# First scores of both row halves in one step over two PSUM banks, the next image's products in a shared bank, and a new order of the second part

## What is computed

```python
q, k, v = split(x @ w_qkv)          # 16 heads of 16
q, k = rotary(q), rotary(k)
scores = q @ k.T * 16 ** -0.5       # per head, 256 x 256, later keys masked
x = x + (softmax(scores) @ v) @ w_out
x = x + sum over the two best experts of gate * (norm(x) @ expert_w[e])
```

## Time and profile before

| | us |
|---|---|
| median of the runs (lowest, highest) | 706.92 (705.33, 708.26) |
| the profiled execution | 706.3 |
| its span from first to last instruction | 704.5 |
| TensorE busy | 614.3 |
| VectorE busy | 468.7 |
| ScalarE busy | 347.4 |
| GpSimd busy | 240.5 |

### The profile page before, as it was taken

How to read it: one execution, slowest core, us unless ns; L and a number is a source line. 1 busy time by engine, 2 the same in 40 slices (tenths; PEclk the granted TensorE clock), 3 DMA queues, 4 the chain that set the end, 5 groups by cost and what they waited for, 6 DMA issues and landing times.

```text
span 704.5 us, 20352 instructions
## 1 busy us (share of the span) xinstructions
PE 614.3 (87%) x8800; PEld 495.7 (70%) x8800; DVE 468.7 (67%) x1032; ACT 347.4 (49%) x549; POOL 240.5 (34%) x257
## 2 busy tenths in 40 slices
PE   6758999999999998566899787999999999989867
PEld 5647888898989898454777355676767676757656
DVE  3686878787787777414576455676777776767545
ACT  5445545655556454228885343636363626262610
POOL 1000103401010103316677446364636465534520
PEclk9868999999999999785999787999999999999987
DMA  8113001300000002002111202020202020200000
GB/s 315 31 62 103 3 3 42 113 17 3 18 2 3 2 3 72 1 0 60 57 35 46 76 1 75 3 76 16 76 1 91 17 76 17 76 17 6 12 16 16
DMA packets 18489, 29.26 MB, mean 42 GB/s; under 512 B 2784, under 2 KB 11232, under 8 KB 18400
## 3 DMA queue, kind: packets, MB, share of 16 engines
q1 hardware_dynamic: 18400, 27.97, 12.3%
HBM read 21.66 MB, written 6.29 MB: 40 GB/s over the span
## 4 chain that ended last, share of the span: by engine, by line
PE 41%; DVE 6%; ACT 4%; POOL 2%; issue 2%; DVEq 0%; POOLq 0%; ACTq 0%
PE ps L197 22%; PE ps L1113 4%; PE ps L1188 4%; PE ps L1116 3%; DVE mx L1465 2%; PE ps L1170 2%; PE ps L1018 2%; PE ps L1148 2%; PE ps L1144 1%; DVE st L1404 1%; POOL rstd L1348 1%; POOL hl L1371 1%; DVE cl_moe L1415 1%; ACT tn_mlp L1237 1%; ACT wide L1281 1%
## 5 line engine op out<-in xcount | busy, mean ns | idle before, releaser
L1385 POOL TENSOR_TENSOR e2l<-prob,e2h 128x1536 f16<-128x1536 f32 x32 | 98.9, 3102 | 35.3 <-ACT e2h L1316 35.3
L1465 DVE TENSOR_REDUCE mx<-ps 128x2 f32<-128x512 f32 (+1 forms) x96 | 66.0, 687 | 52.7 <-PE ps L1116 52.0
L197 PE MATMUL ps<-secondh,ch_moe 128*128 128x256 f16 (+1 forms) x320 | 83.1, 267 | 3.5 <-DVE cl_moe L1415 3.0
L197 PE MATMUL ps<-secondh,cl_moe 128*128 128x256 f16 (+1 forms) x320 | 83.2, 267 | 0.0
L197 PE MATMUL ps<-secondl,ch_moe 128*128 128x256 f16 (+1 forms) x320 | 83.0, 266 | 0.0
L517 PE MATMUL ps<-yh,wconvh 128*128 128x240 f16 (+2 forms) x288 | 78.2, 271 | 4.6 <-POOL yl L677 4.6
L677 POOL TENSOR_TENSOR yl<-y,yh 128x128 f16<-128x128 f32 x32 | 12.6, 426 | 192.9 <-ACT yh L625 192.9
L517 PE MATMUL ps<-yh,wconvl 128*128 128x240 f16 (+2 forms) x288 | 78.1, 271 | 0.0
L517 PE MATMUL ps<-yl,wconvh 128*128 128x240 f16 (+2 forms) x288 | 78.0, 271 | 0.0
L1310 ACT ACTIVATE prob<-ps 128x1536 f32<-128x1536 f32 x32 | 46.3, 1446 | 30.1 <-PE ps L1170 24.9
L1556 DVE SCALAR_TENSOR_TENSOR acc<-ps,gate,acc 128x256 f32<-128x256 f32 x112 | 48.2, 477 | 9.5 <-PE ps L197 9.3
(11 more groups left out here) (220 smaller groups left out, 1996.9 us busy)
## 6 DMA issues: line engine op xcount, KB each, us to landing
weights_stage<-in_second SPq DMA_DIRECT2D x6, 684.0 KB, 4.0
qs<-rope_scratch SPq DMA_DIRECT2D x48, 64.0 KB, 2.3
ks<-rope_scratch SPq DMA_DIRECT2D x48, 64.0 KB, 2.3
weights_stage<-in_wconv SPq DMA_DIRECT2D x6, 384.0 KB, 3.8
xw<-in_xw SPq DMA_DIRECT2D x8, 256.0 KB, 3.5
xc<-in_xc SPq DMA_DIRECT2D x8, 256.0 KB, 2.7
rope_scratch<-rh SPq DMA_DIRECT2D x8, 256.0 KB, 2.3
rope_scratch<-rl SPq DMA_DIRECT2D x8, 256.0 KB, 2.3
```

The lines of the kernel that those rows point to most:

```text
L197: last = nc.tensor.matmul(out_ap, lhs[x], rhs[w], start=done == 0, stop=done == n - 1)
L1385: nc.gpsimd.tensor_tensor(el[n % 2][:], prob[n % 2][:], eh[n % 2][:], ALU.subtract).then_inc(e2_lo, 1)
L1465: nc.vector.tensor_reduce(mx[c % 2][:, q0 // P, h0:h0 + len(heads)], bank(1, 1).rearrange("p (h m) -> p h m", m=keys), op=ALU.max, axis=AX ...
```

## The change

Four things. A `maxima` step now takes the same heads of both halves (head h and head h + 8), in turn, into two banks, `bank(1, 0)` and `bank(1, 1)`, with one mask matmul for each; there are six steps for an image instead of twelve. VectorE takes one maximum over both banks, 1024 columns. The products `q`, `r` and `v` move from `bank(1, 0)`: for image 0 they stay there, image 1 uses `bank(0, 0)`, and all later ones share `bank(0, 3)` with the weighed values; TensorE waits ahead of each of these steps, and of `weigh`, until the last content of the bank has been read. The strings of all engines are new. In TensorE's, while image 4 is attended, the order is `o e q u r a e a c e l r x e a i x x a i x a v x a i x x i s x`.

```diff
     "pe": (
-        "ttttmmwmtwnmwntqwnmrtrtmvwnmqwnmrwnaarawnaaaavaaaqaanseaearaaerevaaiaaiaaiaaisoqeuaearacaelxirxeaxai"
-        "avaxaxaiaxaixxsoqeuaeraaacelirxeaxaiaxaxavaxaixaixxsqoeauearaacelrxeaixaiaxaxavaxaiaxxsixoqeuaearaac"
-        "elixxreaxaiaaxavaxaixaixxsoqeuaeraacaerlixeaxxaiaxaxaiaxaxaixvsoeuaeaacaelixeaxaxaixaxaiaxaxaixsoeue"
-        "celxiexxixxixxxixouclxxxxxxxx"),
+        "tttmmtwwmtnmwntqwrnmtrmwntvwqmnwmaarnrawaavannqserraeaeieaiavaaiisoequaearcelrxeaixiaxxvaxaixxixsoeq"
...
@@
         SCORE_BANKS = [((0, 1, 2, 3), P, 0), ((0, 1), TOK, P), ((2, 3), TOK, P)]
+        SCORE_USES = L1HALF // GH * len(SCORE_BANKS)
+
+        def qkv_bank(c):
+
+            return bank(1, 0) if c == 0 else bank(0, 0) if c == 1 else bank(0, 3)
@@
+            value_bank_read, weighed = [None], [0]
+
+            def value_bank_free():
+
+                freed(pe, o2_done, weighed[0])
+                if value_bank_read[0]:
+                    pe.wait_ge(*value_bank_read[0])
+
             def qkv_channels(c):
 
+                if c == 1:
+                    pe.wait_ge(t1_done, B)
+                elif c == 2:
+                    pe.wait_ge(t2_done, B - 1)
+                value_bank_free()
                 freed(pe, v2_lo, c)
                 pe.wait_ge(ln["norm"][QKV], c + 1)
-                to_channels(bank(1, 0), tn[QKV][0]).then_inc(ln["tr"][QKV], 1)
+                to_channels(qkv_bank(c), tn[QKV][0]).then_inc(ln["tr"][QKV], 1)
+                value_bank_read[0] = n2_lo, c + 1
@@
             def maxima(c, n):
 
-                p, gr, b = c % 2, n // 3, n % 3
-                heads, keys, q0 = SCORE_BANKS[b]
+                p = c % 2
+                heads, keys, q0 = SCORE_BANKS[n % 3]
                 if n == 0:
                     if c == 0:
                         pe.wait_ge(rows_zeroed, 8 * 16)
+                        pe.wait_ge(v2_lo, 1)
                     pe.wait_ge(stacked[p], (c // 2 + 1) * 12 * 16)
                     freed(pe, shift_done, c)
                 else:
-                    pe.wait_ge(max2, c * GROUPS * 3 + n)
-                to = bank(1, 1)
+                    pe.wait_ge(max2, c * SCORE_USES + n)
                 for m, h in enumerate(heads):
-                    rows, at = row_half(gr * GH + h)
-                    nc.tensor.matmul(to[:, m * keys:(m + 1) * keys], qs[p][rows, at, q0:q0 + P],
-                                     ks[p][rows, at, 0:keys], start=m == 0, stop=False)
-                diagonal = to.rearrange("p (h m) -> p h m", m=keys)[:, :, keys - P:keys]
-                nc.tensor.matmul(diagonal, identb[:], maskb[:].unsqueeze(1).to_broadcast([P, len(heads), P]),
-                                 start=False, stop=True).then_inc(scores2, 1)
+                    for g in R2:
+                        rows, at = row_half(g * L1HALF + n // 3 * GH + h)
+                        nc.tensor.matmul(bank(1, g)[:, m * keys:(m + 1) * keys], qs[p][rows, at, q0:q0 + P],
+                                         ks[p][rows, at, 0:keys], start=m == 0, stop=False)
+                for g in R2:
+                    diagonal = bank(1, g).rearrange("p (h m) -> p h m", m=keys)[:, :, keys - P:keys]
+                    last = nc.tensor.matmul(diagonal, identb[:], maskb[:].unsqueeze(1).to_broadcast([P, len(heads), P]),
+                                            start=False, stop=True)
+                last.then_inc(scores2, 1)
@@
                 if gr == 0:
                     pe.wait_ge(v2_lo, c + 1)
                 pe.wait_ge(e2_lo, n + 1)
-                freed(pe, o2_done, n)
+                value_bank_free()
@@
             def maxima(c, n):
 
-                gr, b = n // 3, n % 3
-                heads, keys, q0 = SCORE_BANKS[b]
-                h0 = gr * GH + heads[0]
-                dve.wait_ge(scores2, c * GROUPS * 3 + n + 1)
-                nc.vector.tensor_reduce(mx[c % 2][:, q0 // P, h0:h0 + len(heads)],
-                                        bank(1, 1).rearrange("p (h m) -> p h m", m=keys),
+                heads, keys, q0 = SCORE_BANKS[n % 3]
+                h0 = n // 3 * GH + heads[0]
+                dve.wait_ge(scores2, c * SCORE_USES + n + 1)
+                nc.vector.tensor_reduce(by_half(mx[c % 2])[:, q0 // P, :, h0:h0 + len(heads)],
+                                        bank(1, 0, 2).rearrange("p (g h m) -> p g h m", g=2, m=keys),
                                         op=ALU.max, axis=AX).then_inc(max2, 1)
```

More of the change, by code:

```diff
@@ L1083, in rotate @@
                     last = split_products(
-                        nc, bank(1, 0)[:, m * TOK:(m + 1) * TOK],
+                        nc, qkv_bank(c)[:, m * TOK:(m + 1) * TOK],
                         [([w["wqkv"][:, (j * 2 + h) * C + m * P:(j * 2 + h) * C + (m + 1) * P] for w in (hi, lo)],
@@ L1087, in rotate @@
                 last.then_inc(qk2_done, 1)
+                value_bank_read[0] = rope_b, c * 4 + 2 * j + 2
             def values(c):
+                value_bank_free()
                 pe.wait_ge(rope_b, c * 4 + 4)
-                token_product(bank(1, 0), QKV, "wqkv", 4 * C, C).then_inc(v2_done, 1)
+                token_product(qkv_bank(c), QKV, "wqkv", 4 * C, C).then_inc(v2_done, 1)
+                value_bank_read[0] = v2_lo, c + 1
             def row_half(h):
@@ L1132, in attend @@
                         pe.wait_ge(t2_done, B)
+                        pe.wait_ge(v2_lo, 2)
                     pe.wait_ge(shift_done, c + 1)
@@ L1191, in weigh @@
                 last.then_inc(pv2, 1)
+                weighed[0] = n + 1
             def out_channels(c):
@@ L1288, in qkv_channels @@
                 act.wait_ge(ln["tr"][QKV], c + 1)
-                high_part(QKV, bank(1, 0), n2_hi)
+                high_part(QKV, qkv_bank(c), n2_hi)
             def stack(c):
@@ L1301, in values @@
                 nc.scalar.activation(vh[c % 3][:, :, :, 0:L1D],
-                                     bank(1, 0).rearrange("p (t h d) -> p t h d", t=TILES, h=L1H),
+                                     qkv_bank(c).rearrange("p (t h d) -> p t h d", t=TILES, h=L1H),
                                      ACT.Copy).then_inc(v2_hi, 1)
@@ L1438, in qkv_low @@
             def qkv_low(c):
-                low_part(c, QKV, bank(1, 0), n2_hi, n2_lo)
+                low_part(c, QKV, qkv_bank(c), n2_hi, n2_lo)
             def rotate(c, j):
@@ L1444, in rotate @@
                 dve.wait_ge(qk2_done, c * 2 + j + 1)
-                x = bank(1, 0).rearrange("p (m t) -> p m t", m=2)
+                x = qkv_bank(c).rearrange("p (m t) -> p m t", m=2)
                 sin = const("sin").rearrange("p (m t) -> p m t", m=2)
@@ L1455, in values @@
                 dve.wait_ge(v2_hi, c + 1)
[L1456 removed]
+                nc.vector.tensor_tensor(vl[c % 3][:], qkv_bank(c).rearrange("p (t h d) -> p t h d", t=TILES, h=L1H),
                                         vh[c % 3][:, :, :, 0:L1D], ALU.subtract).then_inc(v2_lo, 1)
             def maxima(c, n):
[L1461 to L1466 removed]
+                heads, keys, q0 = SCORE_BANKS[n % 3]
[3 more added lines that the diff above has]
+                                        bank(1, 0, 2).rearrange("p (g h m) -> p g h m", g=2, m=keys),
                                         op=ALU.max, axis=AX).then_inc(max2, 1)
@@ L1473, in shifts @@
                 freed(dve, shift_tr, c)
-                dve.wait_ge(max2, (c + 1) * GROUPS * 3)
+                dve.wait_ge(max2, (c + 1) * SCORE_USES)
                 nc.vector.tensor_tensor(mxh[:], mx[c % 2][:], mx[c % 2][:], ALU.max).then_inc(mx_step, 1)
```

22 lines of the change are left out of this document (11 added, 11 removed).

## The result

The changed kernel takes 674.41 us (median of four runs, 671.33 to 675.64) against 706.66 for the kernel before beside it: a ratio of 0.9541, 95% interval 0.9511 to 0.9572, some 30 to 35 us less. The profiled execution has a span of 671.7 us, 32.8 less than before. I had predicted 680 (669 to 695). Of the five executions in experiment 4, one took 1142.05 us; it is a slow one and stays out of the figures given there.

A forecast was written before the change was run, and what follows sets the result against it. TensorE's queue was taken to bound whole images, waits and a lowered clock the start; 10.4 + 1.7 + 5 x 2.4 + 2.4 = 26.5 us off 706.9 gives 680.4, forecast 680, range 669 to 695.

The forecast's parts named there:

- step 1: Score steps on TensorE: both row halves run at once, so 6.84 us an image becomes 4.34, 2.5 less.
- step 2: Maxima on VectorE: 8.3 us an image becomes 7.3; a step following at once waits 1.32 us instead of 0.79.
- that rival: Reductions take over, 3.2 us per image: 695 us with the start's gain kept, chance 0.12; 705 with it lost, 0.05.
- the wait for a maximum that I counted against the period: Second score step waits for the first reduction, behind the rotation on VectorE: 0.8 us of 1.9 us of waits an image.
- step 3: Shared bank and whole-image order: 1.9 us of waits, period 32.6 to 33 us against 35.3, 2.4 less per image.
- the tightest place: Shared bank passing from rotation to weighed values: rotation's end needed at 16.0 us, comes at 16.3, so no wait.
- step 4: New order at the start: first score step to first `attend` 23 us; `attend` 10.4 earlier, then 1.7 less to `o`.
- the allowance for the clock: First `attend` to image 0's `o`: 25 us by the order, taken as 26.3 because waits may hold the clock down.
- my upper bound: At the start: 12 us less up to image 0's `attend` if the earlier rotation makes the rows land sooner.
- the MLP phase ahead: Work before the first score step: only reordered, nothing removed, so 0 us, bounds 2 either way.

The follow-up runs named there:

- experiment 4: Changed kernel with the first maximum ahead of the first rotation on VectorE in four periods: 674.95 us, ratio 0.9575; run and profiled once more, 676.48 us.
- experiment 1: Changed kernel with each score step cut into its two halves, one after the other, each with its own mask and maximum: 685.58 us, ratio 0.9729.
- experiment 2: Changed kernel with the products of half 0 queued ahead of those of half 1 in a step, instead of in turn: 674.94 us, ratio 0.9573.
- experiment 3: Changed kernel with two 512-column reductions a step in place of one of 1024 columns: 675.52 us, ratio 0.9582.
- experiment 5: Changed kernel with the old order, thinned to six steps, on all engines up to image 0's output: 684.93 us, ratio 0.9712.
- second profile of before: The kernel before, unchanged, run again for a second profile: 706.72 us.
- experiment 6: Kernel before with the new order alone, each new step a pair of old one-bank steps, no shared bank: 767.62 us, ratio 1.0846.
- experiment 7: Kernel before with the new order in paired one-bank steps, plus the next image's products in the weighed values' bank: 769.11 us, ratio 1.0907.

## Why the prediction was right

**TensorE sets the pace, and a step costs what its parts say (step 1).** The price of a step is right to 0.02 us: 0.86 and 0.55 for the two steps, and 2.6 us an image on the queue by experiment 1 against my 2.5. That TensorE sets the pace held for the kernel before, whose five images leave it idle for 6.2 of 176.4 us; after the change it holds for most of an image only, since for 7.4 us of 32.6 the chain of experiment 4 runs on the other engines, and of six score steps made longer in experiment 1 only the four behind the chain cost time (1.7 of 2.6 us). The Trainium skill (TensorEngine Tiling (Array Packing), Key Properties) says that different tiles of the array can load and multiply in parallel and that a change of mode drains TensorE; experiments 1 and 2 agree with both (eight products in the time of four; 0.21 us for one more change to 64 rows and back). The Trainium skill's figure of 81 ns per product (TensorE: Matmul & The Clock Gate, Back-to-back issue gap), weighed in step 1, doesn't hold for these pairs: 0.20 us for eight (0.32 less the 0.12 for leaving) are 25 ns each.

**Reductions (step 2).** Sized right: 1.22 us, and 1.32 for a step that follows at once. They don't bound the kernel: experiment 3 adds 0.4 us of them to an image and the marks stay, so that rival is out. Nor is the wait for a maximum that I counted against the period worth its length: experiment 4 took it away and the period stayed.

**The shared bank and the period (step 3).** The sum came out as laid by hand: 164.65 / 5 = 32.9 us an image, forecast 32.6 to 33, 11.75 less in five images against 12. Its parts are a little off against each other: in the images at full clock TensorE is busy for some 31.2 us, where I had 30.8, and idle for 1.5, where I had 1.9. `r` waits 0.25 (forecast 0.3), the second step 0.5 to 0.9 (0.8), `attend` for exp 0.6 (0.4), and `weigh` not at all for the rotation, the tightest place. The rotated rows are waited for nowhere in these images. What I did not see is that they don't add up: experiment 4 took one away, and others grew by as much, because a chain on other engines ends no sooner.

**The start (step 4).** The first step to the first `attend` takes 23.06 us, forecast 23, at full clock. Two terms were too small. From there to `o` I took 1.7 less, out of fear that the waits would hold the clock down; it was 3.6, and the 24.4 is the 25 that the order alone gave. The step that failed is the allowance for the clock: with 5.8 us of idle time in this stretch it falls only across the end, to 0.62 for four microseconds, and is 0.98 in the mean. Why it held there and not in experiment 5 (0.81, with 6.7 idle) is not shown by a run of its own.

And the first step comes 4.6 us earlier (5.2 against the second profile of before), forecast 3.6. There I had held the step back for the landing of the rows, 377.8 before. That bound was gone: the last loads are issued by 369.25,

```profile
366.51 2.74 SPq L1003 DMA_DIRECT2D ks<-rope_scratch  x6
```

and with the 2.3 to land the rows are there near 371.6, 2.7 ahead of the first step, which waits for nothing. This is the case of my upper bound, an earlier rotation. If the 3.9 us of work that moved behind the step count in full, some 0.7 are left for the MLP phase ahead, put at 0 within 2.

**The sum.** Forecast 26.5. Measured in the profiles, without the first part, 30.3: 3.8 more, of which 1.9 is the allowance for the clock behind the first `attend`, 1.2 the stretch up to it (11.6 against 10.4, nearly all of it the first step), 0.6 the end and 0.3 image 6, less 0.25 in the five images. The remaining 2.5 of the 32.8 lie in the first part, where executions differ by as much.

**Which part does it.** The four changes aren't four gains. Of the total the paired steps are worth 11 to 13 us when taken out (experiment 1, with the new order kept), the start's order 9 to 12 (experiment 5, up to 4.6 of it waits for the shared bank that the old order meets); the one maximum is worth nothing by itself (experiment 3), the new order without the pairs costs 62 (experiment 6), and the shared bank costs some 0.1 us an image in whole images (experiment 7) and is what frees a second bank for the pair. The old order of the whole second part with the new steps was not run, so how much of the period's 2.4 us it would keep stays open.

## What to carry to other kernels

Where a product uses half of TensorE's rows, put products of the other half into the same step: here eight took the 0.32 us of four, and one entry into 64-row work served both. Price a step by the distance of starts in the trace, and a wait only after asking what is late next, since a wait in the shadow of a chain on other engines is worth nothing (experiment 4). An order of work is made for one set of durations; judge it, and the clock that it keeps, together with the steps it was laid for.

## What the hardware showed that was not expected

- Products of the two row halves run at once even when four of one half are queued ahead of four of the other: 0.34 us from the first product to the mask in experiment 2, 0.32 in turns. The Trainium skill (TensorE: Matmul & The Clock Gate, Step-by-step: what each phase is for) says that matmuls stay in program order and only weight loads are pulled ahead; the spacing of starts in experiment 2 doesn't fit that, unless order holds only within a half, which the records can't tell.
- Waits of about a microsecond, one in every pair of score steps, go with a granted clock of 0.84 to 0.96 over whole images in experiment 6, some 20 us in five images beside the waits' own 34.5; after, four of the same images stand at 1.00, with waits of 0.2 to 0.9.
- Executions of the same first part end up to 3.2 us apart (313.7 to 316.9), so a profile of each kernel can differ by that without any cause in the change.
